# Language-model tower on one core: where the token maxima are stored, and when the first slot matrix is copied

## The reference

```python
h = _L0_tok_ref(x, mask, tok_w, pos_w, type_w, gamma, beta)            # embedding, layer norm
h = h + _L0_attn_ref(_layernorm(h), Wq, Wk, Wv)                        # causal attention, one head
h = h + _L0_ffn_ref(_layernorm(h), phi, ln_g, ln_b, w1, b1, w2, b2)    # soft mixture of 64 experts
h = h + _L1_attn_ref(_layernorm(h), w_qkv, w_proj, b_proj)             # 12 heads, rotary positions
h = h + _L1_ffn_ref(_layernorm(h), router_w, w1, b1, w2, b2)           # 8 routed experts
```

```python
phi_n  = phi * rsqrt(sum(square(phi), axis=0) + EPS_NORM)
logits = einsum('bmd,npd->bmnp', x, phi_n)                 # 1024 slots (64 experts x 16) per token
D = softmax(logits, axis=1)                                # over the tokens: what enters a slot
C = softmax(logits.reshape(bsz, m, n * p), axis=-1)        # over the slots: how a token collects
Xs = einsum('bmd,bmnp->bnpd', x, D)
... layer norm, two products per expert with gelu ...
Y = einsum('bsd,bms->bmd', Ys, C)
```

## Time and profile before

| | |
|---|---|
| time, median of 3 runs | 1446.36 us (1445.44 to 1450.07) |
| profiled execution | 1445.35 us |
| its span | 1443.6 us |
| PE busy | 1356.2 us (94%) |
| PE weight loads busy | 1204.4 us (83%) |
| DVE busy | 971.9 us (67%) |
| ACT busy | 936.0 us (65%) |
| POOL busy | 254.6 us (18%) |
| DMA | 221.05 MB in 185812 packets, 29556 of them under 512 B |
| queue of SP (q1) | 152080 packets, 179.52 MB |

### The profile page before, as it was taken

How to read it: one execution, slowest core, us unless ns; L and a number is a source line. 1 busy time by engine, 2 the same in 40 slices (tenths; PEclk the granted TensorE clock), 3 DMA queues, 4 the chain that set the end, 5 groups by cost and what they waited for, 6 DMA issues and landing times. The chain is left out here.

```text
span 1443.6 us, 29745 instructions
## 1 busy us (share of the span) xinstructions
PE 1356.2 (94%) x9101; PEld 1204.4 (83%) x9101; DVE 971.9 (67%) x2952; ACT 936.0 (65%) x2207; POOL 254.6 (18%) x284
## 2 busy tenths in 40 slices
PE   8799999997799999999999999799999999969995
PEld 6678888886689999899999998688898898858885
DVE  7787777554577777777777775388888888632321
ACT  1377777886566666666666665188888888735551
POOL 5321110000011111111111110001221222121344
PEclk9899999998899999999999999999999999989998
DMA  6136665668566666666665665454544546116641
GB/s 203 31 110 149 148 157 143 160 154 220 104 194 194 182 195 196 187 196 185 194 197 185 193 191 184 145 158 132 157 155 148 154 144 202 45 41 148 146 80 18
DMA packets 185812, 221.05 MB, mean 153 GB/s; under 512 B 29556, under 2 KB 152634, under 8 KB 185712
## 3 DMA queue, kind: packets, MB, share of 16 engines
q1 hardware_dynamic: 152080, 179.52, 44.3%
q10 hardware_dynamic: 25952, 33.32, 6.9%
q0 software_dynamic: 7680, 6.95, 2.6%
HBM read 142.36 MB, written 79.90 MB: 154 GB/s over the span
## 5 line engine op out<-in xcount | busy, mean ns | idle before, releaser
L1236 PE MATMUL bank<-e_w,e_h_full 128*128 128x192 f32 x1920 | 324.7, 326 | 0.4
L1236 PEld LDWEIGHTS bank<-e_w,e_h_full 128*128 128x128 f32 x1920 | 310.6, 190 | 1.7 <-ACT e_h_full L1309 1.3
L1309 ACT ACTIVATE e_h_full<-bank,e_b 128x512 f32<-128x512 f32 x240 | 165.1, 688 | 190.6 <-PE bank L60 190.6
L1170 POOL TENSOR_TENSOR e_ln_rstd<-e_ln_var_eps,minus_half 128x4 f32<-128x4 f32 x62 | 62.5, 1008 | 457.8 <-DVE e_ln_var_eps L1359 457.8
L1717 ACT ACTIVATE probs<-bank,head_neg_max 128x128 f32<-128x128 f32 x384 | 134.9, 393 | 7.8 <-DVE head_neg_max L1813 5.6
L1366 DVE TENSOR_SCALAR e_rows<-e_slot_sums,e_ln_mean_var,e_ln_rstd 128x192 f32<-128x192 f32 x248 | 77.5, 376 | 77.6 <-POOL e_ln_rstd L1170 77.6
L1279 ACT ACTIVATE e_x_full<-bank,e_ln_shift,e_ln_gain 128x512 f32<-128x512 f32 x124 | 89.8, 774 | 52.3 <-PE bank L1208 50.0
L995 PE MATMUL bank<-x,dispatch_weights 128*128 128x193 f32 x512 | 96.9, 332 | 11.5 <-ACT slot_stage L844 10.9
L705 DVE TENSOR_REDUCE column_neg_max<-bank 128x4 f32<-128x512 f32 x64 | 44.2, 691 | 80.0 <-PE bank L60 79.0
L60 PE MATMUL bank<-e_x_hi,e_w1hi 128*128 128x512 f32 x216 | 95.4, 442 | 1.1 <-ACT e_h_full L1309 0.5
L1597 PE MATMUL bank<-slot_outputs_then_w_part,combineT 128*128 128x193 f32 x512 | 93.9, 336 | 2.6 <-ACT combineT L1709 2.1
(11 more groups left out here) (271 smaller groups left out, 3105.1 us busy)
## 6 DMA issues: line engine op xcount, KB each, us to landing
slot_sums<-slot_stage SPq DMA_DIRECT2D x64, 386.0 KB
e_slot_sums<-slot_sums SPq DMA_DIRECT2D x64, 386.0 KB, 3.6
slot_outputs<-e_stage ACTq DMA_DIRECT2D x64, 384.0 KB, 3.2
slot_outputs_then_w_part<-slot_outputs SPq DMA_DIRECT2D x32, 768.0 KB
e_w<-in_w SPq DMA_DIRECT2D x64, 288.0 KB, 2.9
slot_logits<-kept_logits SPq DMA_DIRECT2D x32, 512.0 KB
slot_logits<-slot_logits SPq DMA_DIRECT2D x32, 512.0 KB, 3.5
e_w1raw<-in_w SPq DMA_DIRECT2D x80, 192.0 KB, 2.6
```

The source lines that it names most:

```text
L1170: pool.tensor_tensor(rs[u][:], ve[u][:], half[:], ALU.pow).then_inc(rstd_ready, 1)
L1236: last = pe.matmul(ybank(u)[:, j // 2, (j % 2) * D:(j % 2 + 1) * D], hf[:, k, js], w2s[u][:, k, :], start=k == 0, stop=k == MT - 1)
L1309: act.activation(hf[:, m, :], hbank(u, m), act_fn, bias=b1s[:, m, ds(n, 1)]).then_inc(acted, 1)
```

## The change

The maxima are no longer stored per group. When all eight groups are reduced, PE turns the whole tile `T["nm"]` (128 x 32) to 32 rows of 128 in bank 5, ScalarE copies these to a new tile `token_max_rows`, and SP stores them with one transfer of 32 rows of 512 bytes. All of this is at the end of the tower's streams, behind the last slot. PE waits there for the last maximum with four of its eight keep-busy products ahead of it and four behind. SP's later wait is for one store and not for eight.

Apart from that, ScalarE's copy of slot matrix half 0 moves from slot 5 to slot 7 of the turn in which group 1 is embedded; in its stream that is from ahead of the probabilities' eviction to behind the eviction of the first half of the transposed input.

```diff
-        sp.wait_ge(self.T["nm_stored"], 16 * NG)
+        sp.wait_ge(self.T["nm_stored"], 16)
...
-        nm_stored = T["nm_stored"]
+        nm_stored, nm_turned, nm_rows_ready = T["nm_stored"], sem("token_max_turned"), sem("token_max_rows_ready")
+        nm_rows = sb("token_max_rows", [NB, P])
...
-                    if f is not None and s == 1:
-                        fs = slice(f * GB, (f + 1) * GB)
-                        sp.wait_ge(nm_ready, f + 1)
-                        sp.dma_start(T["nm_rows"][fs, :].rearrange("b p -> p b"), T["nm"][:, fs],
-                                     allow_slow_non_contiguous=True).then_inc(nm_stored, 16)
 
                 each_slot(slot)
+                sp.wait_ge(nm_rows_ready, 1)
+                sp.dma_start(T["nm_rows"], nm_rows[:]).then_inc(nm_stored, 16)
...
-                    if (s, e) in ((5, 1), (1, 2)):
+                    if (s, e) in ((7, 1), (1, 2)):
                         k = e - 1
                         act.wait_ge(phi_scaled, k + 1)
                         act.activation(T[f"phi_hi{k}"][:], T[f"phiT{k}"][:], ACT.Copy).then_inc(phi_hi_ready, 1)
 
                 each_slot(slot)
+                act.wait_ge(nm_turned, 1)
+                act.activation(nm_rows[:], b5[0:NB, 0:P], ACT.Copy).then_inc(nm_rows_ready, 1)
...
                 each_slot(slot)
-                keep_busy(pe, T, bank[:, 6, :], 8)
+                keep_busy(pe, T, bank[:, 6, :], 4)
+                pe.wait_ge(nm_ready, NG)
+                pe.transpose(b5[0:NB, 0:P], T["nm"][:], ident[:]).then_inc(nm_turned, 1)
+                keep_busy(pe, T, bank[:, 6, :], 4)
```

## The result

The changed kernel takes 1420.8 us (median of 4 runs, 1418.76 to 1422.77) against 1445.9 us of the kernel before in the same comparison: 25.1 us less, a ratio of 0.9833 with a 95% interval of 0.9814 to 0.9851. The forecast was 1423.7 us, range 1416 to 1433. The profiled execution took 1418.76 us, its span is 1417.0 us, 26.6 us less than the span before. It is the fastest of the four; that of the kernel before, at 1445.35 us, lies near its median, so the profiles are further apart than the medians.

What follows compares the result with a forecast made beforehand. With TensorE at full clock nearly everywhere, waits in the tower and its hand-over to the experts bound the kernel. −0.8 − 7.4 − 9.0 − 5.5 = −22.7 takes 1445.35 to 1422.65; the median, 1.0 above, is 1423.7 us, range 1416 to 1433.

Steps and rivals of the forecast that it cites:

- The holes: After the piecewise stores at 338.89 and 367.00, DMA engines are busy while almost nothing moves, some 8 us each.
- the sum for the first load: First slot-sum load, end of tower: 1.28 MB in 3.4 us plus 1.7 us start and completion; VectorE's statistics 7.2 us earlier.
- The end of the tower: From the first slot-sum load to the experts' begin: −7.2 − 1.2 + 1.0 = −7.4 us.
- Clock: End of the tower: TensorE keeps full clock through turn, keep-busy products and second turn, −1.2 us, bounds 0 and −2.
- Tail: Behind the last maximum: transpose, ScalarE's copy, hand-over and SP's issue add 1.0 us, bounds +0.7 and +1.5.
- The start of the experts: Load lands in 3.6 not 12.3 us: TensorE gains 7.4 of wait and 1.6 of half clock, −9.0 us.
- The covered stores: Six piecewise stores ahead of 338 us, covered by TensorE; only ScalarE's wait for a slot-sum store goes, −0.8 us.
- The moved copy: Group 1: probabilities' eviction starts at 40.6, low part of the transposed input at 47.7 instead of 53.29; −5.5 us.
- with the clock: Upper bound of the gain from moving slot matrix 0's copy, −6.5 us, since TensorE was at half clock in parts there.
- Pieces not the cause: Rival, chance 0.08: low DMA rate belongs to loads reading a tensor still being stored; −5.5 + 1.0 remain, 1441.9 us.
- Slower: Rival, chance 0.03: holes stay, TensorE idles for the last maximum and starts the experts at half clock, +8.8; 1450.7 us.
- Part only: Rival, chance 0.22: hole only shrinks, clock stays low or group 1's lead is lost, each 3 to 5.5 us; near 1430.

Runs made afterwards that it cites:

- group 6: Changed kernel plus one scratch store of 512 4-byte pieces where the kernel before stores the maxima of group 6, ahead of the slot-sum loads: 1428.73 us.
- tail kernels: Changed kernel plus one scratch store of 512 neighbouring 4-byte pieces right behind the rows' store at the end of the tower: 1433.23 us.
- the six stores put back: Changed kernel plus six scratch stores of 512 4-byte pieces, where the kernel before stores the maxima of groups 0 to 5: 1423.66 us.
- the wait filled: Kernel before with 20 instead of 3 keep-busy products in slot 6 of the turn where group 0 attends, copy still at slot 5: 1442.71 us.
- that with 1024 pieces: Changed kernel plus one scratch store of 1024 neighbouring 4-byte pieces at the end of the tower: 1434.67 us (2 runs).
- the rows' store alone: Changed kernel with the copy of slot matrix half 0 back at slot 5 of group 1, so only the maxima's path is changed: 1429.32 us.

## Why the prediction was right, point by point

**The holes.** Their place, their cause by store and their worth were read rightly: at the first load 7.3 us came, forecast 7.2, and the group 6 and tail kernels bring them back one at a time. The forecast needed only the holes' length, which rows 5 and 6 show, and was right by them. What stands behind the length was not as I put it ("512 pieces"): a number of pieces alone doesn't make a hole. By the figure of the Trainium skill (DMA: Bandwidth & Descriptors, the section on measured sizes: some 10.5 ns per packet as the minimum, taken there on loads that GpSimd issues) the sum would have been an estimated −17.5; it was −25.1. Neither a price per packet nor my reading of one fits 2.1 us for 512 of them. In the sum for the first load, the 1.7 us of start and completion stand in no row; the two loads took 5.0 and 5.1 us to land, where the sum gives 5.1.

**The end of the tower.** The sum was right, −7.4 for −7.4, and both small terms in it were too large; that their errors cancel is luck. Clock: −1.2 forecast; from the first statistics to the end of ScalarE's last high part it is 367.96 − 354.23 = 13.7 us before and 350.67 − 337.52 = 13.2 after, −0.6. TensorE did keep its clock (its eight turns take 1.09 us, before 1.97), but what became late next was VectorE's split of the first rows, for which ScalarE waits 0.75 us ahead of its last copies. I had named only TensorE. Tail: +1.0 forecast; from ScalarE's last high part to the experts it is 0.4 before and 0.95 after, so +0.5. The copy takes 0.25 and the issue 0.34, as forecast, but the hand-over between them takes 0.03 and the barrier closes 0.4 behind the last, as before, so the remaining 0.3 us, which I had added for the hand-over, aren't there.

**The start of the experts.** Forecast −9.0, measured −8.2. TensorE's wait for rows is 0.19 us and its clock full, as forecast. The load that is waited for takes 4.3 us to land, before 11.6 (I wrote 3.6 for 12.3; 12.3 was the load behind it). What comes late instead is ScalarE: TensorE waits 1.2 us at 365.35 for the evicted hidden values, because ScalarE takes the rows of expert 2 ahead of them. I wrote "next late is TensorE itself"; one step further on it was ScalarE. Added up: 7.2 of the wait and 1.6 of the clock gained, 0.7 lost at ScalarE (waits of 1.2 us in the changed kernel for 0.5 before), 8.1 of the 8.2. The row of the changed kernel:

```profile
365.35 0.50 PE L60 MATMUL bank<-e_x_hi,e_w1hi 128*128 128x512 f32 x1 [1.20 <-ACT e_h_full L1312]
```

**The covered stores.** −0.8 forecast, −1.2 by place, and the six stores put back cost 1.2 us by place. Right.

**The moved copy.** The order was followed event by event: 40.9 for 40.6, 44.50 for 44.4, 47.69 for 47.7, −5.6 us. The term that failed is the one I left at nothing beyond that: another 2.6 us by the first column. I had it in the bound (−6.5 "with the clock"), too narrow. In the changed kernel the clock is at full from 60 to 68 us:

```profile
60.00:64.00 4.00, 2.17 (x17) 1.95 (x17) 3.71 (x9) 2.13 (x9) 0.00 (x0) 1.00 0.01 2
64.00:68.00 4.00, 3.32 (x18) 2.33 (x17) 3.47 (x13) 2.43 (x7) 0.65 (x1) 1.00 0.00 0
```

and before at 0.67 and 0.50. The 2.6 us are the clock's. From the low part of group 1's input to the first column it is 19.8 and 19.2 us in the two kernels with the copy unmoved and the wait unfilled, 16.7 in that with the wait filled, and 17.2 to 17.6 in ten of the eleven with the copy moved. The eleventh, that with 1024 pieces, takes 20.4: its clock is 0.50 from 56 to 64 us, although TensorE was busy just as long ahead of it, from 52 to 56 us, as in the kernel with only the copy moved (2.46 and 2.47 us). So the move brings these 2.6 us in most executions and not in all. The clock isn't full everywhere with the copy moved either: TensorE's first products of the next step run at half clock (0.79 us at 49.09).

How the 5.6 us up to the low part split is a matter of counting, since order and clock overlap there: the filled wait alone, in the old order, gives 1.9 of them (51.37 for 53.29). By the first column the eleven kernels with the copy moved stand at 64.0 to 65.3, but for the one at 68.5, and those with it unmoved and unfilled at 73.0 and 74.9. This lead is also why the experts begin at 351.62 and not near 355.

**The last 1.6 us.** Between the combine phase's begin and the end, where nothing was changed, the changed kernel is 1.6 us shorter in the profiled execution. This is scatter: its second product over the slots ran 16 steps in 4.28 us, mostly at half clock, in the profile before (925.49 us) and in 2.86 at full clock in that after (900.42 us), each with 1.47 us of idle time just ahead. The short one is the exception: in the other twelve executions the product takes 4.38 to 5.49 us. From the phase's begin to the end of the last phase's table load the 14 profiled executions take 384.0 to 388.8 us, without regard to what was changed in them. The medians of the runs, 25.1 apart, hold less of it than the spans, 26.6 apart.

**The rivals.** "Pieces not the cause" was ruled out by the rows' store alone and by the tail store. "Slower" needed TensorE idle for as long as from 349 to 352 us; it stood 1.43 us for the last maximum and kept its clock. The mechanism isn't empty, though: with one more store at the tail and otherwise the same order, the clock was 0.50 from 352 to 354 us in the kernels with 16-byte pieces, with 512 pieces side by side and with one row of them (0.53 and 0.80 in the two with pieces apart, 1.00 in that with 4096), for two to three us of the experts' first products, and not for the 8.8 that I had priced. "Part only" didn't come, since the low clock and the lost lead that it priced didn't appear.

## What to carry to other kernels

A small store can cost nothing where it is issued and 8 us where it isn't looked for: compare the landing times of the same load at different places in the kernel, look at what its queue, and the other queues, were given just before, and price the store only where somebody waits for what is queued behind it. Where a column must go to a row of memory, turn it on chip first, or set its elements 64 bytes apart if the reader can take that; storing it once but still element by element gave back 1.5 us here. Where a chain has an idle stretch of TensorE, ask what its clock does behind the stretch before pricing only the wait.

## What the runs showed of the hardware

512 pieces of 4 bytes from one tile took 11.3 us to land when they were neighbours in memory, 2.3 us at 64 bytes' distance, and 2.1 at 512 bytes'; the same 2 KB in 128 neighbouring pieces of 16 bytes took 3.0 us, and 32 rows of 512 bytes 1.4 us. More rows of neighbours cost little more: 8.0, 11.3, 12.6 and 22.1 us for 1, 4, 8 and 32 rows of 128 pieces. I had expected a price per piece. The small packets themselves were sent within 0.8 us in either case; the packets of the transfers behind them waited, on ScalarE's queue too.

TensorE's granted clock isn't the same function of its idle time in each execution. At the begin of the combine phase, with the same instruction order and nearly the same gaps (0.45, 1.61 and 1.47 us, and 0.62, 1.31 and 1.47), it fell to 0.50 in one profile and stayed at 1.00 in the other. The product behind the last of these gaps took 2.86 us in that one profile and 4.28 to 5.49 us in the other 13, so a difference of up to 2.6 us at one such place can be this alone.
